# Column sums over one block instead of two: a second ScalarE write of h, an accumulating DMA, onehot copies on ScalarE, and another order in batches 0 to 2

## The reference

```python
# x: (32, 256, 1024) f32; adj: (256, 256); b1, b2: (256,)
h = jnp.maximum(_layernorm(x, axis=-1), 0.0)
x = x + _L0_gnn_ref(h, adj, b1, adj, b2)

def _L0_gnn_ref(x, W1, b1, W2, b2):
    adj = _construct_adj(x, 8)             # (1024, 1024) for every batch
    xr = jnp.swapaxes(x, 1, 2)
    h = jax.nn.relu(_gc(xr, adj, W1, b1))
    h = _gc(h, adj, W2, b2)
    return jnp.swapaxes(h, 1, 2)

def _construct_adj(x, k):
    fv = x.mean(axis=1)                    # column means of h: one vector of 1024
    nf = fv / jnp.linalg.norm(fv, axis=1, keepdims=True)
    sim = nf[:, :, None] * nf[:, None, :]
    _, idx = jax.lax.top_k(sim, k + 1)     # neighbours of each node, the first left out
    idx = idx[..., 1:]
    ...                                    # set ones there, make symmetric, ones on the diagonal

def _gc(x, adj, W, b):                     # degree-normalised mean over the neighbours
    deg = adj.sum(axis=2, keepdims=True)
    h = x @ W.T + b
    return jnp.einsum('bij,bjh->bih', adj / deg, h)
```

## Time and profile before

| | |
|---|---|
| median of 3 runs | 503.58 us |
| the profiled execution | 504.29 us |
| its span | 502.5 us |
| TensorE (PE) busy | 478.3 us (95%) |
| VectorE (DVE) busy | 375.1 us (75%) |
| ScalarE (ACT) busy | 350.0 us (70%) |
| GpSimd (POOL) busy | 363.1 us (72%) |
| chain that ended last, by engine | PE 86%, DVE 5%, ACT 3%, DMA 3% |
| column_sums on that chain (L592) | 5% |
| group_twin on DVE (L847) | 20.4 us, 16 instructions of 1275 ns |

### The profile page before, as it was taken

One profiled execution on the slowest core, in us unless ns is written; L12 is line 12 of the kernel. 1 busy time (PEld: TensorE's weight loads), 2 busy tenths in 40 slices (PEclk: granted clock), 3 DMA queues, 4 the chain that ended last, 5 costly groups with the idle time before them and its releaser, 6 DMA issues.

```text
span 502.5 us, 7464 instructions
## 1 busy us (share of the span) xinstructions
PE 478.3 (95%) x2434; PEld 327.7 (65%) x2434; DVE 375.1 (75%) x956; ACT 350.0 (70%) x723; POOL 363.1 (72%) x343
## 2 busy tenths in 40 slices
PE   1997799899999999999999999999999999999996
PEld 0255556667776677767776677767777677777774
DVE  5989688988977898778877898878877675533334
ACT  4766698757877777777777777787777755556651
POOL 0356547957779687886888687896888687898883
PEclk9999799999999999999999999999999999999999
DMA  8992473556656465655656465664453244444424
GB/s 323 357 378 85 134 273 116 226 184 238 248 204 247 162 253 217 236 227 206 247 197 261 162 251 217 242 252 175 179 202 134 104 165 154 169 167 168 167 85 167
DMA packets 27718, 102.75 MB, mean 204 GB/s; under 512 B 2080, under 2 KB 2592, under 8 KB 27680
## 3 DMA queue, kind: packets, MB, share of 16 engines
q1 hardware_dynamic: 27296, 101.23, 53.5%
q0 software_dynamic: 384, 1.05, 0.6%
HBM read 68.72 MB, written 33.55 MB: 204 GB/s over the span
## 4 chain that ended last, share of the span: by engine, by line
PE 86%; DVE 5%; ACT 3%; DMA 3%; issue 1%; POOL 1%; SPq 0%; DVEq 0%; ACTq 0%; POOLq 0%
PE ps L629 48%; PE ps L635 22%; PE aux L592 5%; PE ps L657 4%; PE aux L688 3%; DMA xin<-x 2%; PE aux L616 1%; ACT hb L336 1%; PE aux L579 1%; DMA xg<-x_t,rows 1%; DVE res L943 1%; DVE onehot L847 1%; DVE stats L761 1%; PE aux L603 1%; POOL h_lo L491 1%
## 5 line engine op out<-in xcount | busy, mean ns | idle before, releaser
L502 POOL TENSOR_TENSOR r_lo<-r,r_hi 128x512 fp32r<-128x512 f32 x128 | 162.8, 1294 | 45.7 <-ACT r_hi L403 44.0
L491 POOL TENSOR_TENSOR h_lo<-hb,h_hi 128x512 fp32r<-128x512 f32 x128 | 164.0, 1295 | 7.5 <-ACT h_hi L366 7.4
L943 DVE SCALAR_TENSOR_TENSOR res<-ps,bias,res 128x512 f32<-128x512 f32 x128 | 90.1, 746 | 71.9 <-PE ps L664 71.9
L629 PE MATMUL ps<-r_hi,w_hi 128*128 128x512 f32 x256 | 109.0, 426 | 1.8 <-ACT r_hi L395 1.8
L629 PE MATMUL ps<-h_hi,w_hi 128*128 128x512 f32 x256 | 105.4, 412 | 0.4 <-DVE res L943 0.4
L629 PE MATMUL ps<-r_hi,w_lo 128*128 128x512 f32 x256 | 102.0, 399 | 0.0
L629 PE MATMUL ps<-h_hi,w_lo 128*128 128x512 f32 x256 | 101.0, 395 | 0.0
L336 ACT ACTIVATE hb<-xin,nmean,rstd 128x1024 f32<-128x1024 f32 x64 | 78.7, 1230 | 8.7 <-DVE nmean L782 8.7
L386 ACT ACTIVATE r<-ps,beta 128x512 f32<-128x512 f32 x64 | 43.4, 684 | 58.8 <-PE ps L657 56.5
L380 ACT ACTIVATE r<-ps,beta 128x504 f32<-128x504 f32 x64 | 43.5, 679 | 56.6 <-PE ps L657 52.3
L761 DVE BATCH_NORM_STATS2 stats<-xin 128x6 f32<-128x512 f32 x128 | 79.0, 677 | 3.6 <-DMA xin<-x 3.6
(11 more groups left out here) (100 smaller groups left out, 548.1 us busy)
## 6 DMA issues: line engine op xcount, KB each, us to landing
res<-x SPq DMA_DIRECT2D x32, 1024.0 KB, 4.9
out<-res SPq DMA_DIRECT2D x31, 1024.0 KB, 4.0
xin<-x SPq DMA_DIRECT2D x30, 1024.0 KB, 7.1
xin<-x SPq DMA_DIRECT2D x4, 512.0 KB, 5.0
out<-res SPq DMA_DIRECT2D x4, 256.0 KB, 2.1
w<-w_t SPq DMA_DIRECT2D x1, 256.0 KB, 9.0
cst<-small SPq DMA_DIRECT2D x1, 229.5 KB, 6.8
xg<-x_t,rows POOLq DMA_INDIRECT x8, 5.6
```

The source lines that it names most:

```text
L491: last = nc.gpsimd.tensor_tensor(h_lo[:, kf, n], hb[:, b % NH, kf, n], h_hi[:, kf, n].bitcast(F32), ALU.subtract)
L502: last = nc.gpsimd.tensor_tensor(r_lo[:, kf, n], r[:, kf, n], r_hi[:, kf, n].bitcast(F32), ALU.subtract)
L629: nc.tensor.matmul(bank[m][:], wt[:, kf, m * P:m * P + P], mov[:, kf, n], start=(kf == 0 and wt is w_hi), stop=False, skip_group_check=True)
L943: nc.vector.scalar_tensor_tensor(res[:, b % NR, m, n], bank[m][:], bias2[:, m:m + 1], res[:, b % NR, m, n], ALU.add, ALU.add).then_inc(out ...
```

## The change

1. **h's first row block is written twice.** From batch 12 on (group 3), ScalarE runs `both(b)`: normalise(b, 0), then the same activation of row block 0 into the new buffer h_sum (one slot for each batch of a group), then normalise(b, 1). POOL then issues `fold(b)`, a DMA from its queue that adds row block 1 of hb onto h_sum. `column_sums(k)` for k >= 3 waits for all four folds and runs over h_sum alone: 8 matmuls instead of 16. It also stands later, behind layer2(t, 1).
2. **The halves of the one-hot tile are copied on ScalarE** (`twin`), no longer computed on VectorE (`group_twin`).
3. **Order of the steady iterations.** On ScalarE, take_sums moves behind split_h(t+2, 0), zeros behind split_r(t+1, 1); in t mod 4 = 2 `both` moves from the end of the iteration to its middle; the root moves to the end and is one batch further ahead (t+10). On VectorE moments and scales are one batch further ahead too, and scales moves to the very end of the iteration, just ahead of the next table.
4. **Another order in batches 0 to 2** on ScalarE and VectorE.

```diff
+            def both(b):
+                normalise(b, 0)
+                if b >= 3 * G:
+                    e = b % RB
+                    act.wait_ge(fv_done, 2 * (b // G))
+                    nc.scalar.activation(h_sum[:, b % G], xin[:, b % NX, 0], ACT.Relu, bias=nmean[:, 0, e:e + 1],
+                                         scale=rstd[:, 0, e:e + 1])
+                normalise(b, 1)
+            def twin(k, i):
+                act.wait_ge(counted, k + 1)
+                nc.scalar.activation(onehot[64 - 64 * i:128 - 64 * i, k % 2, 1], onehot[64 * i:64 * i + 64, k % 2, 0],
+                                     ACT.Copy).then_inc(onehot_ready, 1)
...
+            def fold(b):
+                pool.wait_ge(h_ready, b + 1)
+                nc.gpsimd.dma_start(h_sum[:, b % G], hb[:, b % NH, 1], accum_op=ALU.add).then_inc(folded, 16)
...
+                if t > 4 and t % G in (1, 2) and t + LEAD < NB:
+                    fold(t + LEAD)
                 split_r(t + 1, 0)
...
+                if t > 5 and t % G == 2 and t + LEAD + 1 < NB:
+                    fold(t + LEAD + 1)
                 split_r(t + 1, 1)
                 if t >= 0 and t + 2 < NB:
                     split_h(t + 2, 1)
+                if t > 3 and t % G == 0 and t + LEAD < NB:
+                    fold(t + LEAD)
...
             def column_sums(k):
-                pe.wait_ge(h_ready, G * k + G)
+                if k < 3:
+                    pe.wait_ge(h_ready, G * k + G)
+                else:
+                    pe.wait_ge(folded, 16 * G * (k - 2))
                 pe.wait_ge(beta_ready, k)
+                blocks = KF if k < 3 else 1
...
-                if group_at(t, 0) is not None:
+                if group_at(t, 0) == 2:
+                    column_sums(2)
+                layer2(t, 1)
+                if t > 3 and group_at(t, 0) is not None:
                     column_sums(group_at(t, 0))
-                layer2(t, 1)
...
             for t in range(3, NB):
-                ahead = t + LEAD + 1
+                ahead = t + LEAD + (2 if t > 5 else 1)
...
                 finish(t, 1)
-                if ahead < NB:
+                if t < 6:
                     scales(ahead)
...
+                if t > 5 and ahead < NB:
+                    scales(ahead)
```

More of the change, by code:

```diff
@@ L420, in _ @@
             split_h(1, 1)
+            twin(0, 0)
             normalise(5, 0)
@@ L431, in _ @@
             for t in range(LAST):
[L432 to L434 removed]
+                if t in (1, 3):
+                    normalise(t + LEAD, 0)
+                    normalise(t + LEAD, 1)
                 relu(t + 1, 0, 0)
@@ L439, in _ @@
                     root(7)
-                if group_at(t, 0) is not None:
-                    take_sums(group_at(t, 0))
+                if t == 6:
+                    root(t + LEAD + 1)
                 if t + 2 < NB:
@@ L449, in _ @@
                     root(LEAD)
-                if t == 1:
-                    root(LEAD + 2)
-                if 2 < t < NB - LEAD - 1:
+                if t == 2:
+                    normalise(LEAD + 2, 0)
+                    normalise(LEAD + 2, 1)
+                if 2 < t < 6:
                     root(t + LEAD + 1)
+                elif t > 5 and t % G == 2 and t + LEAD + 1 < NB:
+                    both(t + LEAD + 1)
+                if group_at(t, 2) is not None:
+                    twin(group_at(t, 2), 0)
                 relu(t + 1, 1, 0)
@@ L456, in _ @@
                 split_r(t + 1, 1)
+                if group_at(t, 0) is not None:
+                    zeros(group_at(t, 0))
                 if t == 0:
@@ L460, in _ @@
                     split_h(t + 2, 1)
+                if t == 2:
+                    twin(1, 0)
+                    twin(1, 1)
+                if group_at(t, 2) is not None:
+                    twin(group_at(t, 2), 1)
                 if t == 0:
                     zeros(1)
+                    twin(0, 1)
                     normalise(LEAD, 0)
@@ L465, in _ @@
                     root(LEAD + 1)
-                elif t + LEAD + 1 < NB:
-                    normalise(t + LEAD + 1, 0)
-                    normalise(t + LEAD + 1, 1)
-                if t == 1:
-                    root(LEAD + 3)
+                elif t < 3:
+                    root(t + LEAD + 1)
+                else:
+                    if t > 5 and t + LEAD + 2 < NB:
+                        root(t + LEAD + 2)
+                    if (t < 6 or t % G != 2) and t + LEAD + 1 < NB:
+                        both(t + LEAD + 1)
         @block.gpsimd
@@ L979, in _ @@
             join(7)
+            table(0)
+            scales(7)
+            finish(0, 0)
             spreads(8, 0)
-            group_twin(0, 1)
-            table(0)
-            finish(0, 0)
             spreads(8, 1)
-            scales(7)
             join(8)
             spreads(9, 0)
-            spreads(9, 1)
             finish(0, 1)
             scales(8)
+            spreads(9, 1)
             join(9)
+            class_terms(1)
+            top_first(1)
+            scales(9)
+            table(1)
             spreads(10, 0)
-            class_terms(1)
+            finish(1, 0)
+            top_next(1)
+            top_best(1)
+            top_rows(1)
+            finish(1, 1)
+            class_terms(2)
             spreads(10, 1)
-            top_first(1)
-            top_next(1)
-            scales(9)
             join(10)
-            table(1)
-            top_best(1)
-            finish(1, 0)
-            top_rows(1)
-            spreads(11, 0)
-            spreads(11, 1)
-            finish(1, 1)
+            table(2)
+            top_mark(1)
             scales(10)
-            join(11)
-            top_mark(1)
-            class_terms(2)
-            table(2)
             finish(2, 0)
@@ L1018, in _ @@
             group_counts(1)
-            group_twin(1, 0)
-            group_twin(1, 1)
-            scales(11)
+            spreads(11, 0)
             finish(2, 1)
+            spreads(11, 1)
+            join(11)
+            class_terms(3)
             group_degrees(1)
             group_factors(1)
-            class_terms(3)
             group_gathered(1)
             group_sources(1)
+            scales(11)
             for t in range(3, NB):
-                ahead = t + LEAD + 1
+                ahead = t + LEAD + (2 if t > 5 else 1)
                 if t > 3 and (t + 1) % G == 0 and t < LAST:
@@ L1044, in _ @@
                     moments(ahead)
+                if t == 6:
+                    scales(t + LEAD + 1)
                 if group_at(t, 0) is not None:
```

31 lines of the change are left out of this document (13 added, 18 removed).

## The result

515.65 us median (514.86 to 518.09, 4 runs) against 503.58: ratio 1.025, 95% interval 1.0225 to 1.0272. The change makes the kernel 12.1 us slower; 6.1 were forecast. The profiled execution took 514.86, its span is 513.1: 10.6 more than before. (It is the shortest of its four, and the profiled one of before lies 0.7 above its median; that is the difference to 12.1.)

The account below looks back on a forecast made before the run. TensorE was taken to bound the kernel from iteration 3 on. Groups 3 to 6 at +4.8, group 7 at +0.5 and batches 0 to 2 at +0.8 made +6.1: 509.7 us, range 499 to 518.

Parts of the forecast that it names:

- What bounds: TensorE is the chain from iteration 3 to the end without a gap, busy in all 57.00 us of a group.
- part 1: column_sums, groups 3 to 7: half of the matmuls go, 5 x 1.79 = 8.9 us off TensorE.
- Part 2: ScalarE's longer chain in t mod 4 = 1 and 2 makes TensorE wait 1.9 us a group.
- Part 3: VectorE behind the later column sums: the next table is late, TensorE waits 1.1 us a group (0.8 to 1.3).
- Part 4: The accumulating DMA (fold) lands in 6.0 us (2.8 to 9): no wait in four groups, 0.6 in the last.
- The room: Time from the issue of a group's last fold to its column sums: 6.1 us, 5.4 in group 7.
- the third rival: Folds land late: at 9 us column sums wait in every group, 524 us, at 7.5 517; chance 0.18.
- the estimate from the Trainium skill: The fold priced at 2.0 us and bytes over 436 GB/s: 3.2 us, without the 0.6 wait, time 509.0.
- Part 5: New order in batches 0 to 2: +0.8 us in all, with -2 and +3 as ends.
- The rest ahead of table(0): TensorE's 3.32 us wait for table(0) shrinks by about 1.9, as VectorE has less ahead of it.
- The named loss: layer2(2, 0) waits for r_lo(2, 0), behind gather(1) on POOL: the gain turns into about 1 us lost.
- Sum: Groups 3 to 6 +4.8, group 7 +0.5, with batches 0 to 2 +6.1 us: 510.4 profiled, 509.7 median.

Follow-up runs that it names:

- h: The changed kernel with the twins of groups 2 on back on VectorE, where the kernel before has them: 512.5 us, ratio 1.0187.
- half_moved: The kernel before with column sums of groups 3 to 7 over row block 0 alone and moved behind layer2(t, 1): 500.6 us, ratio 0.9941.
- load_waits: The changed kernel with SyncE's load of res in t mod 4 = 2 held back until the group's folds have landed: ratio 1.0172.
- q: Kernel before with the new early order, twin(0, 1) and group 1's gather put later, root(11) and scales(11) earlier: 503.7 us, ratio 0.9993.
- steady_only: The changed kernel with the old order of batches 0 to 2 and the load of res held back for the folds: 509.5 us, ratio 1.0115.
- early: The kernel before with only the new order of batches 0 to 2 and the twins of groups 0 and 1 on ScalarE: 506.5 us, ratio 1.0089.
- p: Kernel before with the new early order, twin(0, 1) behind root(9) and group 1's gather behind r_lo(2, 0): 506.1 us, ratio 1.0036.
- no_fold: The changed kernel without its 20 accumulating DMAs, row block 1 left out of the sums of groups 3 to 7: 512.7 us, ratio 1.0177.

## Why the prediction was right in direction and wrong in size

- **What bounds, part 1.** Right. TensorE is the chain from iteration 3 on, and half of the column sums is worth 1.71 a group (1.79 said).
- **Part 2.** Right: a group costs 1.2 without the fold, and -0.65 with parts 1 and 3 alone, so part 2 is 1.85 (1.9 said), with ScalarE busy for 49.0 of a group (50 said). The wait for src is 1.14 of it, read from starts (1.1 said). The second write took 1.13 (1.1 said), the twin 1.08 (0.95). The twin's share is shown by h in three groups; the second write was not tried alone.
- **Part 3.** Right: 1.06 (1.1 said), and 0.61 in the last group (0.6 said), shown by the moved run, which changes nothing else.
- **Part 4.** The step that failed is "I take 6.0, the gathers' median and a little for the size: no wait in four groups, 0.6 in the last". The room was as said: 6.16 us from the issue of a group's last fold to the column sums (6.1 said), 5.5 in the last group (5.4). What failed is one landing for all groups. The folds that count landed in 4.8, 5.4 and 5.5 in three groups, in 6.9 in group 5 and in 8.5 in the last, so the waits were 0.67 and 3.00: 3.1 of the 4.5 that were missing in the profiled execution. For the last, load_waits shows the cause: a load issued 0.33 us ahead. The median of 8.4 is that of all 20 folds, and 15 of them have more room than they need. So the third rival (landing 7.5 to 9, with a wait in every group) was right in the last group alone. I had asked what a DMA costs, not which 1 MB transfer SyncE issues at that moment. By the estimate from the Trainium skill (3.2) the miss would have been larger; the shortest accumulating landing, 4.5 without a neighbour, is still above it, while the shortest plain copy (2.9) is below.
- **Part 5.** The other term that was mis-sized is "I take +0.8, with -2 and +3 as ends": 1.96 in the profiled execution, 3.3 between the medians of the early order alone and before. The rest ahead of table(0) shrank as said, from 3.32 to 1.49. The named loss (r_lo behind the gather) came too, with a lag of 1.85 at class_terms(2), but at class_terms(3) 0.16 are left of it. What counts is the end of VectorE's list: tab(3), and normalise(11) behind scales(11), which I named without a price. q, which mends this as well as the twin and the gather, is even with the kernel before. The clock, which I had named beside the late fold only, costs where it falls in column_sums(2) and cost nothing at 74 to 78 us. What makes it fall was not tried by itself and stays open.
- **Sum.** The lag of 10.56 is 4.4 more than the 6.15 I had: 3.1 by the fold, 1.2 by batches 0 to 2, 0.2 by all the rest. For parts 1 to 3 I had 4 x 1.2 - 0.1 = 4.7; with the 0.7 of one fold wait that makes 509.0, and steady_only measured 509.5. Of the 12.1 in the medians the rest is the fold (3.6 by the ratios, from 1.0249 to 1.0177) and the early order (2.1 in the profile of early, 3.3 between its medians).

## What to carry to other kernels

Price a new DMA by what its engines do in that very stretch: list the transfers that other queues issue within a few microseconds of it, and where one of them falls together with a DMA that an engine waits for, move that neighbour first. Look at the landing that is waited for, not at the median of all. A wait that is absorbed one iteration later costs nothing, so follow a moved step to the last instruction of its list, not to the first wait. Room on an engine is counted per iteration: the same addition costs up to 1.8 a group (2.3 less the 0.57 of half_moved) or nothing, by the place it has in the list.

## What the runs showed of the hardware

- A 512 KB accumulating DMA within SBUF takes twice the DMA engines' time of a copy of the same bytes (10.3 against 5.1% of the span). It landed in 4.5 us at best, with no other transfer beside it, in 8.5 beside a 1 MB load issued 0.33 us ahead, and in 12.3 at worst.
- TensorE's granted clock fell to 0.57 in a 4 us stretch behind a single rest of 1.85 us (early), and to 0.50 behind rests of 0.69 and 0.35 (p). Behind rests as long it also stayed at 1.00 (no_fold, and the changed kernel behind 3.00).
- A stretch of low clock cost nothing where TensorE waited for another engine right behind it (18.29 us with it, 18.25 without), and 1.4 to 2.8 us where it fell in column_sums(2) (4.99 to 6.44 for 3.64).
- VectorE's addition of two SBUF operands took 1.18 us at the least and 2.16 at the most, beside POOL's subtractions. The Trainium skill ("SBUF — State Buffer", Who interferes with whom) has one port pair for which a VectorE instruction with two SBUF inputs and a GpSimd instruction that reads SBUF contend, the loser blocking; the spread agrees with it, but no run here took POOL's work away.
